# Splitting the attention weights by columns, projecting k and q first, and making TensorE's early unread work from products of zeros

## The reference

```python
q = elu(x @ Wq.T) + 1; k = elu(x @ Wk.T) + 1; v = x @ Wv.T      # 16 heads of 16, x layer-normed
kv_sum += k_i v_i^T; k_sum += k_i                               # a scan over the tokens
out_i = (q_i kv_sum) / (q_i . k_sum + EPS);  x += out @ Wo.T    # causal linear attention
x += routed(norm(x)) + mlp(norm(x), Wg_s, Wu_s, Wd_s)           # 8 experts, 4 chosen, one shared
```

## Time and profile before

| | before |
|---|---|
| median of 3 runs | 1035.76 us (1035.69 to 1036.71) |
| profiled execution, its own time | 1034.56 us |
| its span, first to last instruction | 1032.8 us |
| TensorE busy | 1007.5 us (98%) |
| VectorE busy | 870.3 us (84%) |
| ScalarE busy | 422.9 us (41%) |
| GpSimd busy | 537.7 us (52%) |
| chain that ended last, share by engine | PE 86%, DVE 5%, DMA 4%, ACT 2%, POOL 1% |

### The profile page before, as it was taken

The page is one execution under the profiler, slowest core; times in us unless marked ns, Lnnn a source line. Parts: engine busy times, 40 slices in busy tenths (PEclk is TensorE's granted clock), DMA queues, the critical chain, the costliest instruction groups (busy, mean ns, idle before and its releaser), DMA issues.

```text
span 1032.8 us, 22213 instructions
## 1 busy us (share of the span) xinstructions
PE 1007.5 (98%) x8437; PEld 858.1 (83%) x8437; DVE 870.3 (84%) x1855; ACT 422.9 (41%) x750; POOL 537.7 (52%) x440
## 2 busy tenths in 40 slices
PE   6889999999999999999999999999999999999997
PEld 5667888888888888888888888888888888888886
DVE  5988989898988889889898998889889798877564
ACT  5755343434434244343434434344343434422222
POOL 5763545646454564445546444564545546343653
PEclk9999999999999999999999999999999999999999
DMA  5011425335252543425335252543424335241411
GB/s 204 2 47 43 105 60 136 81 103 113 58 138 63 147 89 103 97 64 136 75 103 113 59 141 65 147 83 103 102 64 136 71 105 114 58 116 42 124 61 64
DMA packets 235162, 96.49 MB, mean 93 GB/s; under 512 B 161713, under 2 KB 217521, under 8 KB 235057
## 3 DMA queue, kind: packets, MB, share of 16 engines
q1 hardware_dynamic: 235056, 95.07, 36.0%
HBM read 66.60 MB, written 28.44 MB: 92 GB/s over the span
## 4 chain that ended last, share of the span: by engine, by line
PE 86%; DVE 5%; DMA 4%; ACT 2%; POOL 1%; issue 1%; SPq 1%; DVEq 0%; ACTq 0%; POOLq 0%
PE bank L1003 54%; PE y_bank L1003 18%; PE bank L1112 6%; PE bank L1128 4%; PE bank L1099 2%; PE bank L1142 1%; DMA x_dram<-blocks 1%; DMA expo<-x_dram 1%; POOL xa_lo L720 1%; DMA cw_all<-in_w_qkvo 1%; DVE et L971 1%; PE bank L1154 1%; SPq L555 0%; DMA cw_all<-cw_dram 0%; DVE blocks L847 0%
## 5 line engine op out<-in xcount | busy, mean ns | idle before, releaser
L1003 PE MATMUL bank<-xt_hi,wg_hi 128*128 128x512 f32 x576 | 237.2, 412 | 3.1 <-DVE et L971 2.4
L1003 PE MATMUL bank<-xt_hi,wg_lo 128*128 128x512 f32 x576 | 228.0, 396 | 0.0
L1003 PE MATMUL bank<-xt_lo,wg_hi 128*128 128x512 f32 x576 | 227.8, 395 | 0.0
L746 POOL TENSOR_TENSOR h_lo<-et,h_hi 128x512 fp32r<-128x512 f32 x142 | 181.0, 1291 | 89.4 <-ACT h_hi L696 89.1
L743 POOL TENSOR_TENSOR et<-et,cw_all 128x512 f32<-128x512 f32 x124 | 163.5, 1338 | 111.9 <-DVE et L977 93.7
L874 DVE TENSOR_TENSOR scores<-bank,cst 128x512 f32<-128x512 f32 x240 | 152.7, 682 | 35.3 <-PE bank L1112 29.0
L1003 PE MATMUL y_bank<-wd_hi,h_hi 128*128 128x256 f32 x576 | 164.9, 286 | 0.2 <-POOL h_lo L746 0.2
L1003 PE MATMUL y_bank<-wd_lo,h_hi 128*128 128x256 f32 x576 | 162.0, 281 | 0.0
L1003 PE MATMUL y_bank<-wd_hi,h_lo 128*128 128x256 f32 x576 | 161.4, 280 | 0.0
L1003 PEld LDWEIGHTS bank<-xt_hi,wg_hi 128*128 128x128 f32 x576 | 108.3, 188 | 41.7 <-issue 16.9
L696 ACT ACTIVATE h_hi<-et 128x512 fp32r<-128x512 f32 x144 | 86.1, 624 | 117.1 <-POOL et L743 60.2
(11 more groups left out here) (136 smaller groups left out, 1871.5 us busy)
## 6 DMA issues: line engine op xcount, KB each, us to landing
cw_all<-cw_dram SPq DMA_DIRECT2D x124, 256.0 KB, 3.9
x_dram<-blocks SPq DMA_DIRECT2D x112, 128.0 KB, 3.4
out_y<-x_mid SPq DMA_DIRECT2D x32, 256.0 KB, 4.6
x_in<-in_x SPq DMA_DIRECT2D x15, 512.0 KB, 5.3
num_t<-x_dram SPq DMA_DIRECT2D x15, 512.0 KB, 4.1
expo<-x_dram SPq DMA_DIRECT2D x13, 512.0 KB, 4.0
k_dram<-blocks SPq DMA_DIRECT2D x52, 96.0 KB, 2.6
k_tok<-k_dram SPq DMA_DIRECT2D x13, 384.0 KB, 3.4
```

The source lines that it names most:

```text
L746: nc.gpsimd.tensor_tensor(h_lo[:, i % HR, :], et[:, i % ET, :], h_hi[:, i % HR, :].bitcast(f32), ALU.subtract).then_inc(h_lo_done, 1)
L1003: ins = nc.tensor.matmul(dst, l, r, start=first and n == 0, stop=last and n == 2, skip_group_check=shared)
```

## The change

Three edits, all in the start.

1. Pieces 0 and 1 are cut by columns: piece 0 holds the columns of q and k (all input features), piece 1 those of v and o. A piece is still 512 KB, but in each partition it now is two runs of 512 values (2 KB) where it was one of 1024 (4 KB), in memory and in `wa_hi`, `wa_lo`. k and q of batch 0 wait for piece 0 alone, v and wo for piece 1.
2. TensorE's list has k.0.0 and q.0.0 ahead of v.1.0, and ScalarE's takes v.1.0 out behind q.0.0.
3. The unread work ahead of the turns is 22 products of the zeroed tile `cw` with itself; it waits for GpSimd's third memset (L702) and no longer for the constants, for which the turns now wait.

```diff
-WARM = 16
+WARM = 22
 FIRST PE:
-        turn.0.0 turn.1.0 warm.17.0 v.1.0 k.0.0 q.0.0 v.0.0 k.1.0 q.1.0 scores.0.0 k_turn.0.0 scores.1.0
+        turn.0.0 turn.1.0 warm.17.0 k.0.0 q.0.0 v.1.0 v.0.0 k.1.0 q.1.0 scores.0.0 k_turn.0.0 scores.1.0
 FIRST ACT:
-        piece.0.0 piece.1.0 turn.1.0 turn.0.0 piece.2.0 v.1.0 piece.3.0 k.0.0 piece.4.0 piece.5.0 q.0.0 k.1.0
+        piece.0.0 piece.1.0 turn.1.0 turn.0.0 piece.2.0 piece.3.0 k.0.0 piece.4.0 piece.5.0 q.0.0 v.1.0 k.1.0
...
-        PIECES = [(w_qkvo[:, kc], 4 * D, wa_hi[:, kc], wa_lo[:, kc]) for kc in range(KC)]
+        PIECES = [(w_qkvo[:, :, n * 2 * D:(n + 1) * 2 * D], KC * 2 * D, wa_hi[:, :, n * 2 * D:(n + 1) * 2 * D],
+                   wa_lo[:, :, n * 2 * D:(n + 1) * 2 * D]) for n in range(2)]
...
+        def stage(n):
+            flat = staging[n % NS][:, 0:PIECES[n][1]]
+            return flat.rearrange("p (k n) -> p k n", k=KC) if n < KC else flat
...
+            pe.wait_ge(zeros_set, 3)
+            zeros = cw[:, :, :].rearrange("p s e -> p (s e)")
+            for n in range(WARM):
+                nc.tensor.matmul(bank[BANK["turn", 0]][:, 0:P], zeros, zeros, start=True, stop=True)
             pe.wait_ge(small_in, 48)
-            for n in range(WARM):
-                nc.tensor.transpose(bank[BANK["turn", 0]][:, 0:P], ident, ident)
...
                 elif name in ("v", "wo"):
                     if b == 0:
-                        for n in range(KC):
-                            wait_split(pe, n)
+                        wait_split(pe, 1)
...
                 elif name in ("k", "q"):
                     if b == 0:
-                        for n in range(KC):
-                            wait_split(pe, n)
+                        wait_split(pe, 0)
```

More of the change, by code:

```diff
@@ L527, in _ @@
                         wait_split(sp, i - NS)
-                    src, cols, _, _ = PIECES[i]
-                    sp.dma_start(staging[i % NS][:, 0:cols], src).then_inc(staged[i], 16)
+                    sp.dma_start(stage(i), PIECES[i][0]).then_inc(staged[i], 16)
                 elif name == "cw_store":
@@ L577, in weights_high @@
             def weights_high(n):
-                _, cols, hi, _ = PIECES[n]
                 act.wait_ge(staged[n], 16)
-                nc.scalar.activation(hi, staging[n % NS][:, 0:cols], ACT.Copy).then_inc(split_hi, 1)
+                nc.scalar.activation(PIECES[n][2], stage(n), ACT.Copy).then_inc(split_hi, 1)
             act.wait_ge(zeros_set, 1)
@@ L706, in _ @@
                     pool.wait_ge(split_hi, i + 1)
-                    _, cols, hi, lo = PIECES[i]
-                    nc.gpsimd.tensor_tensor(lo, staging[i % NS][:, 0:cols], hi.bitcast(f32), ALU.subtract)\
+                    _, _, hi, lo = PIECES[i]
+                    nc.gpsimd.tensor_tensor(lo, stage(i), hi.bitcast(f32), ALU.subtract)\
                         .then_inc(split_lo, 1)
@@ L784, in _ @@
                 if name == "piece":
-                    _, cols, hi, lo = PIECES[i]
+                    _, _, hi, lo = PIECES[i]
                     dve.wait_ge(split_hi, i + 1)
-                    nc.vector.tensor_tensor(lo, staging[i][:, 0:cols], hi.bitcast(f32), ALU.subtract)\
+                    nc.vector.tensor_tensor(lo, stage(i), hi.bitcast(f32), ALU.subtract)\
                         .then_inc(attn_split, 1)
```

## The result

The changed kernel takes 1039.76 us (median of 6 runs, 1038.23 to 1040.59) against 1035.72 us before (6 runs, 1034.35 to 1036.71). The ratio is 1.0043 with a 95% interval of 1.0032 to 1.0054: **4 us slower**, where 0.6 us faster was forecast and 1036.6 was the end of the range. The profiled execution has 1040.21 us and a span of 1038.4 against 1032.8.

The account below looks back on a forecast made before the run. TensorE's products bound the kernel from 100 us on, so only the front could shift: -0.55 us on TensorE and ScalarE, -0.9 on GpSimd, taken as -0.6; 1035.76 - 0.6, rounded to 1035.1 us, range 1033.4 to 1036.6.

Parts of the forecast that it names:

- What bounds the kernel: Whole span: TensorE's products fill it from 100 us on, 925.01 of 930 us; the change only moves that stretch's beginning.
- Products of zeros: TensorE's unread work ahead of the turns: 44 records from 1.43 to about 8.6 us, no gain or cost by itself.
- the cover: Behind the turns of x: 1.4 us of slack; only turns ending after about 11.8 us would move anything.
- Cut by columns: Loads of pieces 0 and 1: runs of 2 KB cost 0 to 0.18 us for the two, taken as 0.1.
- The first projection and ScalarE: Front: TensorE starts at 13.96, 0.55 us earlier; ScalarE's k.0.0 leaves from 16.0, 1.7 us earlier; scores.0.0 starts at 24.0.
- The step that failed is GpSimd's: GpSimd's three wg_lo follow the second at 16.9 and end at 24.0; VectorE's cum could end 0.9 us earlier.
- rival B: Between 30 and 100 us the shift is lost, as where GpSimd and VectorE instructions meet: 1035.8 us; chance 0.2.
- A: The forecast itself: the front's shift of 0.55 to 0.65 us reaches the end, 1034.4 to 1035.8; chance 0.58.
- C: More arrives, by better VectorE and GpSimd meetings or ScalarE's 1.65 us at q.0.0: 1034.1 us; chance 0.13.
- D: Products of zeros do not lift the clock; projections start 0.6 us late: 1037.4 us (1036.4 to 1038.6); chance 0.08.
- E: Products of zeros give back 4.5 us of projections at half pace: 2.25 us more than forecast, 1032.9; chance 0.01.
- q.1.0 follows without the 0.98 us: TensorE, front: k.1.0 ends at 21.27 and q.1.0 follows without its earlier 0.98 us wait for q.0.0's bank.

Follow-up runs that it names:

- statistics late: Changed kernel with batch 1's layer-norm statistics moved on VectorE from ahead of k.0.0 to behind k.1.0: ratio 1.0010 to the kernel before, 1037.03 us.
- power ahead: Changed kernel with batch 1's power (rstd1.0.1) moved ahead of piece 3 in GpSimd's list: ratio 1.0014 to the kernel before, 1036.92 us.
- quarters: Changed kernel with GpSimd's low parts of pieces 2 to 5 written by four instructions of 256 columns each: ratio 1.0008 to the kernel before, 1037.11 us.
- the one without zeros: Changed kernel with its 22 products of zeros replaced by the 16 turns of the identity: ratio 1.0040 to the kernel before.
- the one without the gap: Kernel before with ScalarE's copies of pieces 3 and 4 both ahead of v.1.0, nothing else changed: ratio 1.0042, 1040.06 us.
- zeros alone: Kernel before with only its unread work ahead of the turns made of 22 products of zeros: ratio 1.0019, 1037.41 us.
- the run with the zeros' idle time filled: Kernel before with 22 products of zeros, and 34 instead of 17 unread turns behind the turns of x: ratio 0.9992, 1034.31 us.

## Why the prediction was wrong

*What bounds the kernel*: right. From 100 us on the two kernels are alike, and all that counts happens once, in the front. (The forecast of 1035.1 is 1035.16 by its own sum.)

*Products of zeros*: 44 records from 1.48 as forecast; they end at 9.04, not 8.6, so the pace doubled a little later than reckoned. The turns of x ended at 10.2 (10.3 forecast), and ScalarE took them at 11.94, so the cover held. What the step left out is the idle time that an earlier end opens: on the kernel before it was 2.1 us and cost 1.9 us (ratio 1.0019), all of which came back when it was filled (0.9992). The prediction priced this edit at nothing and looked only at who reads the turns. In the changed kernel it got away with that: the clock stayed at full through the 1.81 us, and without the zeros the kernel is as slow (1.0040).

*Cut by columns*: the second piece landed at 10.97, 0.10 later, as taken, and ScalarE's copies of wa kept 1.06 us. The 0.10 shows nothing of the runs of 2 KB, though: over all 14 profiled executions ScalarE's copy of this piece starts at 10.68 to 11.35 with the old cut and at 10.41 to 11.35 with the new one. Alone the cut is no loss.

*The first projection and ScalarE*: 13.89 against 13.96 forecast, and ScalarE's k.0.0 at 15.99 against 16.0, released by a landing. Up to here every step held. That the first projection came within 0.07 us is luck: in the five experiments that leave this part of the changed kernel alone it starts at 13.33 to 13.82.

***The step that failed is GpSimd's.*** It said that the wg_lo "now follow the second at 16.9 and end at 24.0", and booked this as a gain of 0.9 us, with nothing for what VectorE has to do beside them. They did just that, ending at 23.84, and it was the loss. The gap of 1.19 us on GpSimd looked like waste, but it was the only time in which VectorE could do batch 1's statistics, and k.0.0 and q.0.0 stand behind these in its list. So the prediction's "k.0.0 leaves from 16.0 on" was true for ScalarE's two steps and false for VectorE's third, which came at 24.38. The clue was in a row it quoted: cum took 2.28 us beside GpSimd's pieces and ended 1.1 after them. It priced this as 0.6 us in rival B and never asked which other operations of VectorE lie beside a piece. Putting pieces 3 and 4 ahead of v.1.0 in the kernel before, with no other edit, gives 1.0042.

*The rivals*: A and C did not happen; B had the right mechanism in the wrong place and at a seventh of the size; D is refuted, as zeros did lift the clock and the turns of x ran at full pace; E too. The fall of the clock in idle time of TensorE was no rival at all. That "q.1.0 follows without the 0.98 us" became a wait of 4.50 us, and the clock fell in it.

*How the 4 us add up.* In the profiled executions q.1.0 starts 25.72 - 22.80 = 2.9 us late, by the held statistics. Products at half pace add 2.0 us up to scores.1.0 (32.51 - 27.56 = 4.95 in all). At 50 us, where the chain reaches the long row of products, the lag is 54.76 - 50.40 = 4.4 us. The spans lie 5.6 us apart and the medians 4.0, since the profiled execution of before is 1.2 us below its median and that of after 0.45 above.

Which of the two counts? Neither alone costs the 4 us. With the 4.5 us filled, q.1.0 and scores.0.0 are late by 2.2 and 2.6 us and the clock stays at full: no loss can be told (0.9998). With the statistics late, the power ahead or in quarters, VectorE's k.0.0 starts at 17.1 to 18.7 and the clock falls nevertheless: the granted clock of their 30 executions is 0.993 to 0.997, no better than the 0.992 to 0.997 of the changed kernel, and the ratios are 1.0008 to 1.0014. Only where the products behind q.1.0 are both late and at half pace, in the changed kernel, the one without zeros and the one without the gap, is it 1.0040 to 1.0043. How a lag of some 2 us is made up later is not settled: the profile with the 4.5 us filled still lagged by 2.0 us at the long row (52.41) and by 1.2 in the span, inside what its interval allows.

## What to carry to other kernels

Before closing a gap on GpSimd, list what VectorE has to do beside it: small operations that take both inputs from SBUF got through only at the seams of GpSimd's instructions, one or two per seam, and everything queued behind them waited too. Work that moves earlier on TensorE opens an idle stretch behind it; read how long TensorE will stand there, and fill it: in the changed kernel 40 unread turns in a wait of 4.5 us took the ratio from 1.0043 to 0.9998. A gap that looks like waste on one engine can be another's only slot; here one entry of ScalarE's list decided over 4 us.

## What the hardware showed that I had not expected

A small VectorE operation with two inputs in SBUF (128 by 4, 0.15 us of work) lasted as long as the GpSimd instruction beside it: 2.36 us beside pieces of 1024 columns, 0.59 to 0.70 beside quarters. Operations with one of the inputs in PSUM (kf at 19.09 in the kernel before, 0.69) and the bn_stats (1.41 for four) were not held. The Trainium skill (GPSIMD Engine Reference, "Key points") names this contention, for instructions with two SBUF inputs and for VectorE's two-port mode; the trace agrees for two SBUF inputs. A TENSOR_SCALAR with one was held as well, 2.38 us in the run without the gap; no row shows in which mode it ran.

In the front the clock of TensorE fell in or right behind idle stretches of 4.50 (changed kernel), 4.24 (the same without zeros), 3.75 (no gap), 2.60 (power ahead), 2.15 (quarters), 2.1 (zeros alone) and 1.80 us (statistics late). It stayed at full in the changed kernel's 1.81 us between 12 and 14, and in the kernel before, whose idle stretches of TensorE from 14 to 30 us are 0.98 us or less. But in the run with the zeros' idle time filled it fell at 28.1 with no stretch over 1 us around it. The clearest case is near the end: in each of the 14 profiled executions TensorE stands idle once for 2.24 to 2.99 us at some point between 1006 and 1019 us, and in six of them the clock fell there for 3.4 us (among them 2.24 and 2.31), in the other eight it did not (among them 2.76 and 2.99). So falls come with idle stretches, but the length of a stretch of 2 to 3 us does not tell whether one comes, and what else it takes stays open. A fall lasted 3.4 or 6.8 us, and 13.7 in the changed kernel without zeros. The Trainium skill's sentence that transposes don't engage the full clock (TensorE: Matmul & The Clock Gate, "Part 4: PE-mode transpose") is against the runs: 40 turns of the identity in 4.5 us kept the clock at full.
